# Attention scores in a fused transformer layer: VectorE writes the second block's causal mask too, and two full products take the place of half-array tiles

## The reference

```python
q = (x @ Wq)...; k = (x @ Wk)...; v = (x @ Wv)...      # x is layer-normed
scores = einsum('bhqd,bhkd->bhqk', q, k) / sqrt(8)
scores = where(causal, -inf, scores)                   # keys after the query
attn = softmax(scores); ctx = einsum('bhqk,bhkd->bhqd', attn, v)
x = x + ctx @ Wo
x = x + experts(layernorm(x))
```

## Time and profile before

| | us |
|---|---|
| median of 3 runs | 591.7 (591.56 to 592.28) |
| the profiled execution, its own time | 592.4 |
| its span in the trace | 590.7 |
| PE busy | 533.6 (90%) |
| DVE busy | 403.1 (68%) |
| ACT busy | 403.0 (68%) |
| POOL busy | 252.3 (43%) |

### The profile page before, as it was taken

One profiled execution on the slowest core, in us unless ns is written; L12 is line 12 of the kernel. 1 busy time (PEld: TensorE's weight loads), 2 busy tenths in 40 slices (PEclk: granted clock), 3 DMA queues, 4 the chain that ended last, 5 costly groups with the idle time before them and its releaser, 6 DMA issues. The chain is left out here.

```text
span 590.7 us, 14103 instructions
## 1 busy us (share of the span) xinstructions
PE 533.6 (90%) x4773; PEld 429.9 (73%) x4773; DVE 403.1 (68%) x1014; ACT 403.0 (68%) x1378; POOL 252.3 (43%) x245
## 2 busy tenths in 40 slices
PE   1599999999999999999999999997059999999996
PEld 1367777777777777777777777776038989989895
DVE  1477888888888888888888887874863234433344
ACT  4698988989889889888888898971215443243230
POOL 4155565555565555555655555560600110110111
PEclk9999999999999999999999999999569999999999
DMA  4585142652251431522513315500020001000001
GB/s 116 159 221 146 33 121 74 214 144 71 74 142 32 110 98 44 142 71 71 143 40 102 112 33 140 144 1 1 1 67 24 20 19 37 20 11 19 19 20 46
DMA packets 49739, 45.82 MB, mean 78 GB/s; under 512 B 4256, under 2 KB 46496, under 8 KB 49696
## 3 DMA queue, kind: packets, MB, share of 16 engines
q1 hardware_dynamic: 48832, 44.60, 27.6%
q10 hardware_dynamic: 864, 0.66, 0.4%
HBM read 26.35 MB, written 18.89 MB: 77 GB/s over the span
## 5 line engine op out<-in xcount | busy, mean ns | idle before, releaser
L385 ACT ACTIVATE prob<-s_ps,neg_max 128x128 f32<-128x128 f32 (+1 forms) x512 | 210.2, 437 | 21.7 <-DVE neg_max L542 20.1
L358 POOL TENSOR_TENSOR probn<-prob,inv 128x1024 f32<-128x1024 f32 x64 | 121.2, 1894 | 45.6 <-DVE inv L546 45.6
L385 ACT ACTIVATION_READ_ACCUMULATOR prob<-s_ps,neg_max 128x1 f32 x512 | 113.9, 223 | 0.0
L351 POOL TENSOR_TENSOR probn<-prob,inv 128x512 f32<-128x512 f32 x64 | 66.6, 1041 | 87.7 <-PE t_ps L659 79.3
L637 PE MATMUL ctx_ps<-probT,v_sb 128*64 128x256 f32 (+1 forms) x1024 | 97.3, 332 | 0.6 <-issue 0.6
L637 PEld LDWEIGHTS ctx_ps<-probT,v_sb 128*64 128x64 f32 x1024 | 63.5, 136 | 27.7 <-issue 9.1
L828 POOL TENSOR_TENSOR y_parts<-y_sb,y_parts 128x512 fp32r<-128x512 f32 x16 | 20.5, 1284 | 137.1 <-ACT y_parts L844 137.1
L473 DVE TENSOR_REDUCE neg_max<-s_ps 128x4 f32<-128x1024 f32 x64 | 76.5, 1196 | 1.3 <-PE s_ps L575 1.3
L650 PE MATMUL misc_ps<-wo_sb,ctxT 128*128 128x128 f32 x512 | 73.9, 288 | 0.0
L650 PEld LDWEIGHTS misc_ps<-wo_sb,ctxT 128*128 128x128 f32 x512 | 61.9, 191 | 10.8 <-issue 10.8
L599 PE MATMUL t_ps<-ident,probn 128*128 128x128 f32 x256 | 62.9, 286 | 1.0 <-ACT probT L423 0.7
(11 more groups left out here) (146 smaller groups left out, 1044.5 us busy)
## 6 DMA issues: line engine op xcount, KB each, us to landing
qT<-q_rows SPq DMA_DIRECT2D x15, 512.0 KB, 4.0
q_rows<-qk_hi SPq DMA_DIRECT2D x32, 128.0 KB, 2.4
q_rows<-qk_lo SPq DMA_DIRECT2D x32, 128.0 KB, 2.4
k_diag_odd<-k_rows SPq DMA_DIRECT2D x32, 128.0 KB, 4.3
k_rows<-qk_hi SPq DMA_DIRECT2D x30, 128.0 KB, 2.4
k_rows<-qk_lo SPq DMA_DIRECT2D x30, 128.0 KB, 2.4
k_diag_even<-k_rows SPq DMA_DIRECT2D x28, 128.0 KB, 4.3
w_raw<-in_L_ffn_w SPq DMA_DIRECT2D x1, 2048.0 KB, 10.4
```

The lines of the kernel that those rows point to most:

```text
L351: nc.gpsimd.tensor_tensor(probn[r][:, 0:HG * P].rearrange("p (i k) -> p i k", i=HG), prob[r][:, 0:HG * P].rearrange("p (i k) -> p i k", i=HG),
L358: nc.gpsimd.tensor_tensor(probn[r][:, HG * P:].rearrange("p (i k) -> p i k", i=HG), prob[r][:, HG * P:].rearrange("p (i k) -> p i k", i=HG ...
L385: last = nc.scalar.activation(prob[r][:, first + i * keys:first + (i + 1) * keys], scores[:, i, :], ACT.Exp, bias=neg_max[:, r, block_, i: ...
```

## The change

- `s1_ps` is laid out by key block: bank 0 holds the first block's keys of all four heads, bank 1 the own block's keys.
- PE makes the scores by two products over all 128 partitions, 512 columns each (L533 and L537 of the changed kernel), in place of L570 and L575. The second waits for a new semaphore, `filled1`. For the very first unit PE writes the mask itself, by one matmul.
- VectorE copies `causal` into bank 1 (L506, the same form of copy as for `s0_ps`). The copy stands between the copy of the last transposes and the maximum of s0, and waits for `exp1`.
- The maximum over s1 and the four exponentials read each head's 256 keys in two pieces, one per bank.
- GpSimd's tables for the half tiles go, 19 instructions at the start.

```diff
-        half_rows = sb("half_rows", [P, 2, P], BF16)
-        half_masks = sb("half_masks", [P, 2, HALF], BF16)
-        causal_halves = sb("causal_halves", [P, 2, HALF], BF16)
-        low_rows_of = sb("low_rows_of", [P, 2, P], BF16)
...
-        s1_ps = ps("s1_ps", [P, HG, T])
+        s1_ps = ps("s1_ps", [P, 2, HG, P])
...
@@ gpsimd
-            def masks():
...
-                        if isinstance(b, int) and b == -2:
-                            masks()
@@ scalar
             def exps(r, block_, scores, keys, first, done):
                 for i in range(HG):
+                    to = prob[r][:, first + i * keys:first + (i + 1) * keys]
                     last = nc.scalar.activation(
-                        prob[r][:, first + i * keys:first + (i + 1) * keys], scores[:, i, :], ACT.Exp,
+                        to if keys == P else to.rearrange("p (k t) -> p k t", k=2), scores(i), ACT.Exp,
...
-                        exps(r1, 1, s1_ps, T, HG * P, exp1)
+                        exps(r1, 1, lambda i: s1_ps[:, :, i, :], T, HG * P, exp1)
@@ vector
                         dve.wait_ge(s1_done, u + 2)
-                        nc.vector.tensor_reduce(out=neg_max[:, r1, 1, :], in_=s1_ps[:, :, :], axis=AX.X,
+                        nc.vector.tensor_reduce(out=neg_max[:, r1, 1, :], in_=s1_ps[:, :, :, :].rearrange("p k i t -> p i k t"), axis=AX.XY,
...
                         nc.vector.tensor_copy(probT[rm][:, 1024:1536], t_ps[rm][:, :]).then_inc(t_dve, 1)
+                    if has(u + 2, UNITS) and has(u + 1, UNITS):
+                        dve.wait_ge(exp1, u + 2)
+                        nc.vector.tensor_copy(s1_ps[:, 1, :, :], bcast(causal[:, :], 1, HG)).then_inc(filled1, 1)
                     if has(u + 2, UNITS):
                         dve.wait_ge(s0_done, u + 3)
@@ tensor
+                        await_count(pe, exp1, u + 1)
+                        nc.tensor.matmul(s1_ps[:, 0, :, :], qT[kb][:, q, P:T], k_diag[kb][:, q, :, 0:P], start=True, stop=True)
+                        await_count(pe, filled1, u + 1)
                         if isinstance(u, int) and u == -1:
-                            pe.wait_ge(halves, 10)
-                        await_count(pe, exp1, u + 1)
-                        tiles = ((slice(0, HALF), 0), (slice(HALF, P), 2))
-                        for rows, i in tiles:
-                            nc.tensor.matmul(s1_ps[:, i:i + 2, :], qT[kb][rows, q, P:T], k_diag[kb][rows, q, i:i + 2, :],
-                                             start=True, stop=False, skip_group_check=True)
-                        for half in range(2):
-                            cols = slice(P + half * HALF, P + (half + 1) * HALF)
-                            for rows, i in tiles:
-                                last = nc.tensor.matmul(s1_ps[:, i:i + 2, cols], half_rows[rows, half, :],
-                                                        bcast(half_masks[rows, half, :], 1, 2),
-                                                        start=False, stop=(half == 1), skip_group_check=True)
+                            nc.tensor.matmul(s1_ps[:, 1, :, :], ident_bf[:, :], bcast(causal[:, :], 1, HG), start=True, stop=True)
+                        last = nc.tensor.matmul(s1_ps[:, 1, :, :], qT[kb][:, q, P:T], k_diag[kb][:, q, :, P:T],
+                                                start=False, stop=True, skip_group_check=True)
                         last.then_inc(s1_done, 1)
```

More of the change, by code:

```diff
@@ L164, in attention @@
         zeroed = sem("zeroed")
-        halves = sem("halves")
         w_hi = sem("w_hi")
@@ L190, in attention @@
         filled0 = sem("filled0")
+        filled1 = sem("filled1")
         inv0 = sem("inv0")
@@ L396, in batch @@
                         await_count(act, normed, u * 2)
-                        exps(r1, 0, s0_ps, P, 0, exp0)
+                        exps(r1, 0, lambda i: s0_ps[:, i, :], P, 0, exp0)
                     if j == 2 and has(b + 2, B):
```

## The result

The changed kernel takes 607.86 us (median of 4 runs, 607.39 to 608.73) against 591.63 us (590.03 to 592.28, 4 runs) for the kernel before: a ratio of 1.028, 95% interval 1.0256 to 1.0304, or 16.2 us more. The forecast was 605.6 us, 13.9 us more. The profiled execution took 608.12 us, its span is 606.2 us.

The account below looks back on a forecast made before the run. PE was taken to bound attention; waiting for the mask copy adds 0.91 us per four units, 0.228 each, times 61 = 13.9 us. Profiled 592.4 becomes 606.3, the median 605.6 us; range 599.5 to 617.0 us.

Parts of the forecast that it names:

- PE waits for the copy in every unit, and loses what lies beyond 1.55 us: Attention: PE waits for the mask copy; copy of transposes to PE's second transpose took 1.55 us before.
- 1.74 us from L503 to PE's second transpose: Usual unit, copy of last transposes to PE's second transpose: 0.60 + 0.67 + 0.06 + 0.31 + 0.10 us.
- The three steps that PE decides: In a four-unit round, delays added along PE's path to its second transpose: 0.19, 0.16 and 0.29 us.
- the step that DVE decides: Four-unit round, entering the unit where DVE is late: copy of transposes falls back 0.27 us through DVE's own queue.
- the late unit: One unit in four: DVE's copy of the transposes doesn't wait for PE, following L535 by 0.60 us.
- Nothing saved on PE counts: Attention: what PE saves by the new products is worth nothing as long as it waits for the mask.
- the 0.10 us: PE's predicted saving per unit: two full products take 0.46 us in place of 0.56 for the part replaced.
- The rule on the pipe of VectorE: Next DVE operation waits for an empty pipe: mask copy 0.09 us later per unit, about 5.5 us in all.
- the two sums: Whole-kernel forecasts: 605.6 us with copies at the shorter distance, 611.1 us under the rule on VectorE's pipe.
- The reads over two banks: Rival: exponentials of s1 over two banks make ACT 0.9 us longer per unit; 615 to 624 us, chance 0.08.
- DVE busier by 31 us: Sign: mask copies add about 31 us to DVE's busy time between 100 and 400 us.
- PE's clock falls: Rival: new gaps of some 0.3 us lower PE's clock in attention; tens of us slower, chance 0.02.

Follow-up runs that it names:

- half the copy: Changed kernel with VectorE's mask copy cut to 256 columns, heads 0 and 1 only: 590.95 us, ratio 0.9992 against the kernel before.
- one place later: Changed kernel with the maximum of s0 put ahead of the mask copy on VectorE: 663.5 us, ratio 1.1226 against the kernel before.
- mask on PE: Changed kernel without VectorE's mask copy; PE adds the mask by a 512-column matmul in every unit: 590.24 us, ratio 0.9997 against the kernel before.
- mask on ScalarE: Changed kernel with the mask copy on ScalarE, behind its exponentials of s1, not on VectorE: 595.7 us, ratio 1.0079 against the kernel before.

## Why the prediction was right

- *PE waits for the copy in every unit, and loses what lies beyond 1.55 us.* Shown: 49 waits in the window, one in each unit, and the time follows the end of the copy in both directions (half the copy 591, one place later 663 us).
- *1.74 us from L503 to PE's second transpose.* Measured 1.80. The copies stand 0.61 us apart, not 0.60; the release takes 0.06 as estimated; the second product takes 0.34 us and not 0.31, which is the term that was most off; the mask copy lasts 0.68 and not 0.67, the transpose takes 0.11 and not 0.10. Unit by unit, the copy of the transposes falls back against the kernel before by 0.25, 0.21, 0.26 and 0.33 us in one round (209.14, 215.09, 221.51, 227.83, 233.77 against 202.45, 208.15, 214.36, 220.42, 226.03). The prediction had 0.19, 0.16, 0.27 and 0.29. The three steps that PE decides are each 0.04 to 0.06 us larger, and the step that DVE decides is right: this is the way from 0.91 to 1.05 us a round, and from 13.9 to 16.2 us.
- *In the late unit VectorE decides.* Shown: at 227.83 L503 follows L499 by 0.60 us with no wait, and it is late by 0.26 us more than the unit before, where the prediction had 0.27.
- *Nothing saved on PE counts.* PE's saving is there only where the mask is not waited for. It is larger than the 0.10 us: with the mask on PE a third matmul of 0.23 us fits into the time of before. The 64-row products also cost at both of their ends: L570 came 0.33 us behind L690, the full product L533 comes 0.23 us behind L651 with the same wait for `exp1` in front of it, and the first transpose takes 0.11 us in place of 0.17.
- *The rule on the pipe of VectorE* (the Trainium skill, "VectorE: DVE Perf Modes", section "The DRAIN you can't avoid"), taken as the prediction took it, would have made the forecast 611.1 us. L506 starts 0.61 us behind L503, which lasts 0.69: the rows go against it in this form. The same section adds that a next operation that is not held starts earlier, and with that the rows agree. The measured 607.9 lies nearly midway between the two sums, but the reason lies on PE's side for the most part, as above.
- *The reads over two banks* were a rival at 615 us or more; they cost nothing (mask on PE: ratio 0.9997).
- *DVE busier by 31 us* in the window: it was 17.8. This sign was wrong as it was put, since the window now holds some two units less. Per unit DVE is busy about 0.58 us more (5.51 in place of 4.93), which is the copy's 0.60.
- *PE's clock falls* didn't happen: it is 1.00 from 100 to 400 us.

## What to carry to other kernels

Work that moves from a full engine to one with idle time is free only if its result is ready when the first engine asks, and here the work alone, with nobody waiting for it, still cost 0.8%. Add up the queue from the last thing that the copy stands behind to the first thing that stands behind it on the waiting engine, and compare with what that path took before. Idle time that is itself a wait for the full engine is no room in front of that engine's next need. Where two engines' rounds are within a few hundredths of a microsecond of each other, the work can be split between them unit by unit, by where each has time; here that made up the loss, and a gain beyond that of the order of the transposes is not shown.

## What was not expected of the hardware

- A product of 512 columns takes 0.23 us start to start in a row of products. Released by a copy that it really waited for it takes 0.33 to 0.34 us, after the 0.21 us of idle time in the changed kernel (210.49 to 210.83) as after the hardly visible wait with half the copy (207.34 to 207.67). Where the mask had been there for long, it took 0.23; one such unit is in the timeline of PE with the mask on ScalarE:

```profile
217.08 0.39 PE L537 MATMUL s_ps<-k_diag_even,qT 128*128 128x512 f32 x1
217.31 0.27 PE L560 MATMUL t_ps<-ident,probn 128*128 128x128 f32 x1
```

  A wait that is met only as PE comes to it costs PE 0.1 us beyond its own length.
- Putting 4 transposes ahead of 8 matmuls of the output projection, not behind them, made the pair 0.05 us shorter in three units of four and the whole kernel 0.5% faster.
- The matmuls over 64 rows of the array cost 0.10 us in front of them and 0.06 us behind them, beyond their own time: 0.33 and 0.17 us, in place of 0.23 and 0.11 around the full products.
